# Two PSUM banks freed at their last readers, and the scale chains of two expert mixtures swapped on GpSimd and ScalarE

## The reference, cut to what matters

```
x = x + attention(layernorm(x))      # gated linear attention, then a 512-wide GELU block
x = x + experts(layernorm(x))        # 8 experts, the best 2 per token: the first mixture
x = x + recurrence(layernorm(x))     # h = tanh(x_t B + h A^T), 16 wide, token after token
x = x + experts(layernorm(x))        # the same experts again: the second mixture

def layernorm(x): return (x - mean(x)) / sqrt(var(x) + 1e-5)
def experts(x):                      # x: tokens x 256
    probs = softmax(x @ router_w.T)
    vals, idx = top_k(probs, 2)
    w = vals / (vals.sum(-1) + 1e-6)
    return sum over the two of (x @ expert_weights[idx] + probs[idx]) * w
```

## Time and profile before

| | |
|---|---|
| median of 3 runs | 1695.19 us (1692.84 to 1696.77) |
| the profiled execution | 1698.78 us, of it 1696.7 us span |
| TensorE matmuls | 1585.6 us busy, 93% of the span |
| VectorE, ScalarE, GpSimd busy | 1267.8, 1035.8, 822.9 us |
| share of TensorE in the chain that ended last | 60% |
| its granted clock, mean over the span | 0.97 of full speed |

### The profile page before, as it was taken

The page is one execution under the profiler, slowest core; times in us unless marked ns, Lnnn a source line. Parts: engine busy times, 40 slices in busy tenths (PEclk is TensorE's granted clock), DMA queues, the critical chain, the costliest instruction groups (busy, mean ns, idle before and its releaser), DMA issues.

```text
span 1696.7 us, 51149 instructions
## 1 busy us (share of the span) xinstructions
PE 1585.6 (93%) x16584; PEld 1331.2 (78%) x16584; DVE 1267.8 (75%) x4557; ACT 1035.8 (61%) x3852; POOL 822.9 (49%) x1293
## 2 busy tenths in 40 slices
PE   4688999999999999999999999999999999998866
PEld 3577788888888888888888888888888888887654
DVE  4566777887788778787877887788778877776644
ACT  4655666666666666666666666766666666655431
POOL 3554454554555455545454554554555545543211
PEclk8798999999999999999999999999999999999978
DMA  5211112111111111011111111111111111110000
GB/s 154 80 57 45 52 57 57 42 39 43 43 56 56 56 51 42 31 51 48 56 56 56 44 36 43 44 55 56 56 54 42 40 43 43 52 51 8 7 6 13
DMA packets 117121, 81.48 MB, mean 48 GB/s; under 512 B 41888, under 2 KB 108096, under 8 KB 116928
## 3 DMA queue, kind: packets, MB, share of 16 engines
q1 hardware_dynamic: 116080, 80.10, 15.6%
q10 hardware_dynamic: 976, 0.54, 0.1%
HBM read 47.06 MB, written 33.55 MB: 48 GB/s over the span
## 4 chain that ended last, share of the span: by engine, by line
PE 60%; issue 12%; POOL 9%; DVE 9%; DMA 5%; SPq 2%; ACT 2%; POOLq 0%; DVEq 0%; ACTq 0%
PE ps L1253 50%; DMA xag<-in_x 3%; PE ps L1270 2%; PE ps L1259 2%; DVE acc L892 2%; DVE hs L860 1%; DMA arow<-att 1%; POOL r L402 1%; PE ps L1299 1%; PE ps L1440 1%; SPq L314 1%; DVE att L949 1%; PE ps L1319 1%; PE ps L1310 1%; POOL res L495 1%
## 5 line engine op out<-in xcount | busy, mean ns | idle before, releaser
L1253 PE MATMUL ps<-we,yT 128*128 128x512 f32 x3072 | 826.7, 411 | 11.5 <-DVE mv_f L879 11.0
L1253 PEld LDWEIGHTS ps<-we,yT 128*128 128x128 f32 x3072 | 539.5, 190 | 117.8 <-DVE mv_f L879 19.5
L566 ACT ACTIVATE h_lead<-ps 48x8 fp32r<-48x8 f32 x1024 | 171.6, 168 | 487.9 <-PE ps L1270 474.1
L860 DVE SCALAR_TENSOR_TENSOR hs<-ps,cst,h_lead 48x8 fp32r<-48x8 f32 x1024 | 224.6, 219 | 249.7 <-ACT ps L567 244.9
L1270 PEld LDWEIGHTS ps<-hs,aT 128*128 128x128 f32 x1024 | 195.1, 191 | 104.9 <-DVE hs L860 73.7
L1270 PE MATMUL ps<-hs,aT 128*128 128x8 f32 x1024 | 208.8, 204 | 42.5 <-DVE hs L860 40.5
L892 DVE SCALAR_TENSOR_TENSOR stage<-ps,coef,stage 128x256 f32<-128x256 f32 x384 | 182.8, 476 | 13.9 <-POOL stage L432 5.6
L892 DVE SCALAR_TENSOR_TENSOR acc<-ps,coef,acc 128x256 f32<-128x256 f32 x384 | 181.8, 474 | 9.3 <-POOL acc L432 4.2
L517 POOL TENSOR_TENSOR orstd<-omean,mhalf 128x32 f32<-128x32 f32 x32 | 174.8, 5461 | 0.2
L567 ACT ACTIVATE ps<-ps 48x8 f32<-48x8 f32 x1024 | 163.1, 159 | 0.0
L430 POOL TENSOR_TENSOR part<-part 128x256 f32<-128x256 f32 x64 | 47.2, 737 | 218.4 <-ACT part L584 216.0
(11 more groups left out here) (185 smaller groups left out, 3197.7 us busy)
## 6 DMA issues: line engine op xcount, KB each, us to landing
arow<-att SPq DMA_DIRECT2D x32, 512.0 KB, 2.8
atx<-arow SPq DMA_DIRECT2D x128, 128.0 KB, 2.8
vrow<-vtok SPq DMA_DIRECT2D x32, 256.0 KB, 2.1
vx<-vrow SPq DMA_DIRECT2D x128, 64.0 KB, 2.0
out<-stage SPq DMA_DIRECT2D x64, 128.0 KB
xin<-in_x SPq DMA_DIRECT2D x62, 128.0 KB
xag<-in_x SPq DMA_DIRECT2D x62, 128.0 KB
stage<-in_experts SPq DMA_DIRECT2D x1, 2048.0 KB, 10.0
```

Source lines behind the costliest of these rows:

```text
L566: a.activation(h_lead[:], ps[0:NB, BANK["RB"], k * B:(k + 1) * B], ACT.Tanh)
L860: v.scalar_tensor_tensor(hs[0:NB, :, k], h_whole, keeps_rest, h_lead[:].bitcast(F32), ALU.mult, ALU.subtract).then_inc(sem("rnn_h"), 1)
L1253: ins = t.matmul(dst, left(lp, c), right(rp, c), start=(n == 0), stop=(n == 3 * chunks - 1))
```

## The change

Four edits, all of order or of a semaphore's name; no instruction is added or removed.

1. `G2_7` now waits for `x1` in place of `mv_m1`, and `G1_0` for `xmid` in place of `mv_f`.
2. GpSimd runs the four instructions of `rstd` for the first mixture ahead of those for the second.
3. ScalarE makes the first tile of `ym2` behind `state_of(7)`, directly ahead of the second tile, and no longer between `state_of(4)` and `state_of(5)`.
4. VectorE takes step 16's split ahead of the first half of `combine(m1, 2)`.

```diff
-    6: [("F1B", 4, ("gT", FB, 4)), ("QK", 2, 'qt'), ("KT", 2, 'ktok'), ("F2", 4, 'mv_m1'),
+    6: [("F1B", 4, ("gT", FB, 4)), ("QK", 2, 'qt'), ("KT", 2, 'ktok'), ("F2", 4, 'x1'),
...
-    7: [("G2_2", 7, ("acc2", 2 * VECTOR_GROUPS, 4)), ("OG", 3, 'oTs'), ("WO", 3, 'mv_f'),
+    7: [("G2_2", 7, ("acc2", 2 * VECTOR_GROUPS, 4)), ("OG", 3, 'oTs'), ("WO", 3, 'xmid'),
...
@@ GpSimd, body @@
                     inner_rstd(c1)
+                if live(it, 4):
+                    target = value(pool, c4)
+                    pool.wait_ge(sem("pads_zero"), 1)
+                    pool.wait_ge(sem("mv_m1"), target)
+                    rstd(m1.mv, m1.r, "m1", c4, True)
                 if live(it, 6):
                     target = value(pool, c6)
                     pool.wait_ge(sem("pads_zero"), 1)
                     pool.wait_ge(sem("mv_m2"), target)
                     rstd(m2.mv, m2.r, "m2", c6, True)
-                if live(it, 4):
-                    target = value(pool, c4)
-                    pool.wait_ge(sem("pads_zero"), 1)
-                    pool.wait_ge(sem("mv_m1"), target)
-                    rstd(m1.mv, m1.r, "m1", c4, True)
@@ ScalarE, body @@
                     state_of(4, c6)
-                if live(it, 7):
-                    act.wait_ge(sem("shift_m2"), c7)
-                    normed(m2.y, m2.x, m2.r, 0).then_inc(sem("ym2"), 1)
                 if live(it, 6):
                     state_of(5, c6)
...
                 if live(it, 6):
                     state_of(7, c6)
+                if live(it, 7):
+                    act.wait_ge(sem("shift_m2"), c7)
+                    normed(m2.y, m2.x, m2.r, 0).then_inc(sem("ym2"), 1)
                 if live(it, 7):
                     normed(m2.y, m2.x, m2.r, 1).then_inc(sem("ym2"), 1)
@@ VectorE, body @@
                     rest(h2Ts, by_chunk("Y1"), "h2Ts")
+                if live(it, 5):
+                    split_state(16, c5)
                 if live(it, 4):
                     dve.wait_ge(sem("moe1"), past((c4 - 1) * GROUPS + 3))
                     combine(m1, 2, 0, BANK["G1_2"], c4)
-                if live(it, 5):
-                    split_state(16, c5)
```

## The result

The changed kernel takes 1716.43 us (median of 6 runs, 1715.51 to 1720.06); the kernel before, run beside it, 1697.05 (6 runs, 1692.84 to 1700.60). The ratio is 1.0113, with an interval of [1.0096, 1.0131]: slower by 19.4 us. Forecast was slower, by 11.3 us, at 1706.5. The loss took the forecast path, but it is larger than forecast, and the time lies above the range's end of 1714.

The account below looks back on a forecast made before the run. TensorE's standstills were taken to bound the kernel. Per round +0.80 at `G1_2` and -0.40 at step 17 gave +0.40, times 27 +10.8 us, with the ends +11.3: 1706.5 us, range from a little below 1700 to 1714.

Parts of the forecast that it names:

- What bounds the kernel: Time is lost or won only where TensorE stands still; rounds have a floor near 48.6 us plus some 0.21 lateness.
- The bank of `G2_7`: `G2_7` starts behind step 5 without a wait, so freeing its bank earlier is worth nothing, at most below 0.1 us.
- The bank of `G1_0` with ScalarE's order: At `G1_0` on TensorE: `lead1` becomes the late input, gaining 0.24 us, bounds 0 to 0.59, swallowed later at `G1_2`.
- GpSimd's order: GpSimd idles 1.35 us waiting for `mv` ahead of the first chain; everything behind it, through `rstd_f`, moves as much.
- The term of 0.80: At TensorE's `G1_2`: GpSimd's slip arrives through `y1` and `hTs`, making it 0.80 us late a round, bounds 0.60 to 0.96.
- The term of -0.40: At step 17 on TensorE: moving step 16's split wins the whole average loss, 0.40 us a round, bounds 0.21 to 0.42.
- The sum: Net +0.40 us a round over 27 rounds, +10.8 us, with the passes before and after together +11.3 us.
- rival C: Places behind step 17 lack slack, adding 0.2 to 0.4 us a round: about 1714 us; chance 0.14.
- The ends: Passes before and after the 27: `G1_0`'s gain -0.5 us, the later first tile of `ym2` +0.5 to +1.5.
- A: Faster: the slip of `y1` does not reach TensorE, both gains stand, 0.64 us a round: 1678 us; chance 0.08.
- B: Smaller slip: GpSimd's port hold is lost, 0.24 us a round less, net +0.16: 1700 us; chance 0.12.
- D: Nothing measurable: the loss at `G1_2` is half, 0.40, and cancels against step 17: 1696 us; chance 0.07.

Follow-up runs that it names:

- part 1 alone: Kernel before with only the banks of `G2_7` and `G1_0` freed at their readers (`x1`, `xmid`): 1693.31 us, ratio 0.9971.
- Part 3 alone: Kernel before with only ScalarE's order changed, the first tile of `ym2` made later: 1709.05 us, ratio 1.0086.
- the kernel without part 2: Changed kernel with GpSimd's order alone put back, second mixture's chain first: 1696.88 us, ratio 0.9993.
- the kernel without part 2 and with the bank of `L2` at its reader: Changed kernel with GpSimd's order put back and the bank of `L2` freed at `lg2`, not `sub2`: 1692.69 us, ratio 0.9990.
- the kernel with banks, split and late `state`: Kernel before with both banks and both router banks freed at readers, step 16's split first, `state` and `elast` behind `rstd_f`: 1697.48 us, ratio 1.0008.

## Why the prediction was right in direction and short in size

**What bounds the kernel.** Right. Every gain and loss of the twelve kernels was read as a distance between two TensorE starts.

**The bank of `G2_7`.** Priced at nothing, and nothing was seen of it apart. No run separates it from the bank of `G1_0`.

**The bank of `G1_0` with ScalarE's order.** Right: 0.25 behind L1284, forecast 0.23. It was swallowed at `G1_2`, as forecast; with parts 2, 3 and 4 left out, the banks are worth 0.3% (part 1 alone). What the step left out is that the tile also moves `mv_f`. Part 3 alone costs 0.86%.

**GpSimd's order.** Right in mechanism and in each station. The idle stretch was forecast at 1.35 and showed as 1.45 us of idle time, the chain 1.37 later than the one that stood there. With that stretch filled the loss vanished. "The second chain ends near 721.8, before ScalarE wants it" was right only through part 3; without it the same order costs 4.7%.

**The term of 0.80.** Right: 0.81 on the average of the 27 rounds. On the same average `rf` came 1.34 late (forecast 1.35), `y1` 1.27 (1.26) and `hTs` 0.99 (1.00). "By the rule the hold passes to `res`" was right in 8 rounds only, with 0.14 us; in 17 the hold fell on the small L409 ahead of it, with 0.28, while `state` gave back 0.23 in both kinds. That the sum stays is so on the average, partly by luck, as the two kinds lie on either side of it: `rf` is 1.41 late in one and 1.27 in the other. Up to L1290 the 0.80 was to stay as it is and grew to 0.83.

**The term of -0.40.** Right at its place (-0.385), and the late transfer was covered in every round. The failing step is the sentence "So the whole average loss at step 17, 0.40 us, is won", taken as the last word on the round: 0.12 is given back at `G1_6` and right behind it, as the bank waits for `sub2`. The sum never priced this gate; rival C had the mechanism, places behind step 17 with too little slack, at 0.2 to 0.4. That `sub2` is the gate is shown by freeing the bank at `lg2`, which took the wait away in the kernel without part 2, where it was 0.26. It was not freed in the changed kernel, and where it was freed later gates gave most of the gain back; so the 0.12 is what the wait measures at its place, not what its removal would bring.

**The ends.** Forecast +0.5 us in all, measured +0.5 at the head and +1.9 behind the last round: another 1.9 us. No experiment moves anything there, so the cause stays open, and it may be chance. Over the fourteen profiled executions the first of the 28 starts lies between 175.59 and 181.44 us and the stretch behind the last between 196.34 and 205.62; two kernels that differ by the release of one bank (the two without part 2) are 3.0 us apart at the head and 2.2 at the end.

The shortfall against the profile adds up: 27 x (0.578 - 0.40) = 4.8 us in the rounds and 1.9 at the ends, 6.7, and 11.3 + 6.7 = 18.0. Of the 0.178 per round 0.12 is the gate at `G1_6`, 0.03 the growth of the slip, 0.015 step 17 and 0.01 is scattered. All these errors have one sign, and the range had let them stand only one at a time. The median missed by more, 9.9 us (1716.43 for 1706.5). The other 3.3 us are the step from the profile to the median: the forecast took off the 3.6 by which the profiled execution of before lay above its median of 3 runs, while the profiled execution of the changed kernel lies 0.3 above its own median.

**The rivals.** A, B and D are out: the slip reached TensorE, and it was not smaller. B had argued from the same port with the opposite sign. C's rounds (net +0.6 to +0.8) are nearly what came, and two thirds of the 0.18 that was added came by its mechanism.

**What was left out.** For a won distance I listed only what holds that same place next. The list has to go on to each gate behind it whose releaser does not move with the gain.

## What to carry to other kernels

In a periodic pipeline a distance won at one TensorE start is worth only what the next gates let through: take each later gate's releaser and ask whether it moves with the gain or stands at its own date. An in-order queue that takes an early-ready piece of work first is doing its consumers a service; putting a late-ready one in front turns that into idle time that every later instruction pays, and the instruction on another engine that waits for the displaced piece must move with it. Freeing a buffer at its last reader rather than at a later result of the same work needs no move at all, and here it was the part that paid, 0.3% by itself.

## What the runs showed of the hardware

The hold between VectorE and GpSimd is far larger than the 0.24 us from which I reasoned, and it goes either way. VectorE's L883, a 128x256 operation on one tensor in SBUF, takes 0.40 us alone and 1.37 beside GpSimd's 128x512 addition, ending 0.16 us behind it; keeping the two apart brought back 0.41. When the two began within 0.02 us of each other, it was GpSimd that stood: 1.51 for 1.27 on the addition, 0.47 for 0.19 on a 128x2 operation. An L409 that began 0.04 us ahead came through in 0.19, and the `res` behind it took 1.42 for 1.28. Size is no protection: VectorE's L922, two inputs of 128x2, took 0.67 us in the kernel without part 2 and with the bank of `L2` at its reader, beside GpSimd's L432 of 128x256 (735.83 to 736.56), and 0.15 in a quiet stretch of the kernel with banks, split and late `state`. No run moves L922 or L432, so this last cause is read from the rows only:

```profile
735.91 0.67 DVE L922 TENSOR_TENSOR two<-p 128x2 f32<-128x2 f32 x1
```

```profile
725.57 0.15 DVE L922 TENSOR_TENSOR two<-p 128x2 f32<-128x2 f32 x1
```

The Trainium skill (SBUF — State Buffer, "SBUF: two separate sides") has the two engines share a port pair that whichever starts first locks for its whole instruction while the other fully blocks. The runs agree that one stands for the other, as `y1` at 1.37 and at 0.41 us shows with nothing changed but when GpSimd's addition ran. They do not show a full block: beside an L883 of 0.40 us GpSimd lost 0.24 to 0.28. And in the round from 723.77 it was L409 that lost, though its row starts 0.02 us first.
